# Gate and up projections of a routed feed-forward block: twelve plain products against one step of Strassen's scheme

## What is computed

```python
x = x + tanh(g_xattn) * attention(layernorm(x), ctx, ctx)     # 32 query heads, 8 key heads of 16
x = x + tanh(g_ffn) * ffn(layernorm(x))

# ffn, t = 8192 tokens, h = 512, FS = 1408, 32 experts of F = 352, 4 per token, 64 tokens per expert at most
shared = (silu(x @ Wsg) * (x @ Wsu)) @ Wsd * sigmoid(x @ Wse)
probs = softmax(x @ Wr); topw, topi = top_k(probs, 4), normalised
expert e, on its first 64 tokens: (silu(xe @ Wg[e]) * (xe @ Wu[e])) @ Wd[e], weighted, added to the token's row
```

## Time and profile before

| | |
|---|---|
| runs of the kernel | 2306.56 us median of 3 (2306.51 to 2308.84) |
| the profiled execution, its own time | 2309.02 us |
| its span in the profile | 2307.2 us |
| instructions in the profile | 43358 |

### The profile page before, as it was taken

One profiled execution on the slowest core, in us unless ns is written; L12 is line 12 of the kernel. 1 busy time (PEld: TensorE's weight loads), 2 busy tenths in 40 slices (PEclk: granted clock), 3 DMA queues, 4 the chain that ended last, 5 costly groups with the idle time before them and its releaser, 6 DMA issues.

```text
span 2307.2 us, 43358 instructions
## 1 busy us (share of the span) xinstructions
PE 2250.8 (98%) x13953; PEld 1735.8 (75%) x13953; DVE 1150.2 (50%) x2218; ACT 763.7 (33%) x1312; POOL 593.1 (26%) x1395
## 2 busy tenths in 40 slices
PE   6999999999997999999999999999999999999999
PEld 5777777777776877777777777778777777777777
DVE  6999999999997723222232222223222232223232
ACT  5888888888883101010110101101010110101010
POOL 5677777777763100000000000000000000000100
PEclk9999999999998999999999999999999999999999
DMA  3555555555553133222223221222222223222321
GB/s 83 147 146 144 146 146 150 144 144 146 143 159 127 10 120 118 85 84 80 65 94 107 84 80 64 80 81 101 84 84 80 68 93 105 84 80 92 121 67 43
DMA packets 269455, 235.14 MB, mean 102 GB/s; under 512 B 120545, under 2 KB 196321, under 8 KB 269410
## 3 DMA queue, kind: packets, MB, share of 16 engines
q1 hardware_dynamic: 265058, 221.89, 32.0%
q0 software_dynamic: 4352, 12.65, 1.9%
HBM read 161.88 MB, written 71.57 MB: 101 GB/s over the span
## 4 chain that ended last, share of the span: by engine, by line
PE 68%; DVE 1%; DMA 0%; issue 0%; DVEq 0%; POOLq 0%
PE acc L1128 7%; PE p_u L1144 7%; PE p_u L1145 7%; PE p_u L1146 7%; PE acc L1130 7%; PE acc L1129 7%; PE p_g L1144 7%; PE p_g L1146 7%; PE p_g L1145 7%; PE p_x L1176 2%; PE p_y L1163 2%; PE p_x L1163 2%; PE p_x L1154 0%; DMA rows<-out_dram 0%; PE p_y L1169 0%; DVE rows L1108 0%
## 5 line engine op out<-in xcount | busy, mean ns | idle before, releaser
L1062 DVE TENSOR_TENSOR act_f<-p_u,act_f 128x512 f32<-128x512 f32 x176 | 121.7, 692 | 984.9 <-PE p_u L1146 984.8
L967 ACT ACTIVATE act_f<-p_g 128x512 f32<-128x512 f32 x176 | 105.3, 598 | 1215.8 <-PE p_g L1146 1194.8
L561 DVE TENSOR_REDUCE negmax<-p_max 128x8 f32<-128x1024 f32 x256 | 312.6, 1221 | 43.6 <-PE p_max L713 43.6
L1128 PE MATMUL acc<-wd_h,hh 128*128 128x512 f32 x704 | 279.5, 397 | 0.0
L1144 PE MATMUL p_u<-xh,wgu_h 128*128 128x512 f32 x704 | 274.8, 390 | 3.6 <-DVE act_f L1062 3.6
L1144 PE MATMUL p_g<-xh,wgu_h 128*128 128x512 f32 x704 | 275.7, 392 | 0.0
L1145 PE MATMUL p_u<-xl,wgu_h 128*128 128x512 f32 x704 | 274.6, 390 | 0.0
L1146 PE MATMUL p_u<-xh,wgu_l 128*128 128x512 f32 x704 | 274.4, 390 | 0.0
L1129 PE MATMUL acc<-wd_l,hh 128*128 128x512 f32 x704 | 274.3, 390 | 0.0
L1130 PE MATMUL acc<-wd_h,hl 128*128 128x512 f32 x704 | 274.2, 390 | 0.0
L1146 PE MATMUL p_g<-xh,wgu_l 128*128 128x512 f32 x704 | 274.2, 390 | 0.0
(11 more groups left out here) (142 smaller groups left out, 3465.5 us busy)
## 6 DMA issues: line engine op xcount, KB each, us to landing
ew<-in_L_ffn_Wg_dram SPq DMA_DIRECT2D x32, 704.0 KB
ew<-in_L_ffn_Wu_dram SPq DMA_DIRECT2D x32, 704.0 KB
xs<-in_x_dram SPq DMA_DIRECT2D x64, 256.0 KB, 2.7
xres<-in_x_dram SPq DMA_DIRECT2D x64, 256.0 KB, 2.8
out_dram<-x SPq DMA_DIRECT2D x64, 256.0 KB, 2.7
xn_rows<-xn SPq DMA_DIRECT2D x64, 256.0 KB, 3.0
xn_cols<-xnT SPq DMA_DIRECT2D x64, 256.0 KB, 3.3
rows<-out_dram SPq DMA_DIRECT2D x16, 1024.0 KB, 5.2
```

The costliest lines, as they stand in the source:

```text
L561: nc.vector.tensor_reduce(negmax[c // 2][:, :].rearrange("p (g c i) -> p c i g", g=2, c=2)[:, c % 2, :, :], p_max[:, :, :].rearrange("p a ...
L1062: nc.vector.tensor_tensor(act_f[:, :], p_u[:, :], act_f[:, :], ALU.mult).then_inc(h_done, 1)
L1128: mm(acc[:, j, :], a[:, t], wd_h[:, f, :], start=(f == 0), stop=False)
```

## The change

Gate and up are taken together as one product of 2x2 blocks: the weights are four blocks (rows: first and second half of the 512 inputs; columns: gate and up), and so are the tokens (features in halves, tokens in halves of 256). Instead of the eight block products (12 + 12 matmuls of 512 columns per chunk) seven are made, with sums of blocks (the Winograd form of Strassen's step):

- weights: A11, A12, A21, A22 and S3 = A11-A21, S1 = A21+A22, S2 = S1-A11, S4 = A12-S2; seven blocks are kept (S1 takes A21's place), each split in high and low;
- tokens: B11, B21, B22 and T1 = B12-B11, T3 = B22-B12, T2 = B22-T1, T4 = B21-T2, each split in high and low.

Each product has 2 contraction blocks x 3 terms = 6 matmuls of 256 columns. The outputs are completed partly by accumulation in PSUM and partly by copies on ScalarE (`term`, `sum16`) and additions on VectorE. The seven split weight blocks need more SBUF, so only 5 chunks of them are made in the first stage; the second stage becomes two passes over the 16 tiles (32 tile bodies), 5 chunks in the first pass and 6 in the second, whose weights are loaded and split between and beside the passes. Rows and tokens are loaded twice, rows stored twice. The down product of all chunks of a tile now comes at the tile's end, bank by bank, with two banks. Experts start in tile 4; a pair is multiplied in one tile and its rows are added in the next, one pair per two tiles until the last six tiles.

```diff
--- before.py
+++ after.py
+NF = (5, 6)
-WCH = FS // (NB // 2)
+WA = 128 * NF[0]
+WCH = WA // (NB // 2)
+ORDER = (B11, B21, T2, T1, T3, B22, T4)
...
+                def weight_sums(pair):
+                    def w(c):
+                        return wst[:, c, :, :]
+                    pool.wait_ge(wst_in, 32 * (pair + 1))
+                    alone(pool, spare_p)
+                    chain.inc(nc.gpsimd.tensor_tensor(w(S3), w(A11), w(A21), ALU.subtract))
+                    chain.wait(pool)
...
+                    nc.gpsimd.tensor_tensor(w(S4), w(A12), w(S2), ALU.subtract).then_inc(wsum_done, 1)
...
                     if (B - 5).ok:
                         take_top(B - 5)
+                    if weights_split(B):
+                        weight_sums(B.pair)
                     if (B + 2).ok:
                         inverse_root(B + 2, stat1, mv1, ve1, rs1, qraw_done, rs1_done)
...
                     if weights_split(B):
-                        act.wait_ge(wst_in, 32 * (B.pair + 1))
-                        nc.scalar.activation(w_cols(wgu_h, B.pair), wst_cols, ACT.Copy).then_inc(whi_done, 1)
+                        act.wait_ge(wsum_done, B.pair + 1)
+                        nc.scalar.activation(w_cols(ws_h, B.pair), wst_cols, ACT.Copy).then_inc(whi_done, 1)
```

TensorE in the second stage (the old chunk loop and `down` fall away):

```diff
+                def product(T, f, bank, a, b, start):
+                    w_h, w_l = w_slot(T.part, f)
+                    if f == 0:
+                        pe.wait_ge(xlo_done, NX * T.n + ORDER.index(b) + 1)
+                    for k in range(2):
+                        mm(bank, w_h[:, a, k, :], x_h[:, b, k, :], start=start and k == 0, stop=False, skip_group_check=not start)
+                        mm(bank, w_h[:, a, k, :], x_l[:, b, k, :], start=False, stop=False, skip_group_check=not start)
+                        last = mm(bank, w_l[:, a, k, :], x_h[:, b, k, :], start=False, stop=(k == 1), skip_group_check=not start)
+                    return last
+                def last_two(T, f):
+                    s = T.step + f
+                    pe.wait_ge(p5_done, s + 1)
+                    product(T, f, p_c[:, 0:HT], S4, B22, False).then_inc(c12_mm, 1)
+                    pe.wait_ge(c22_done, s + 1)
+                    product(T, f, p_a[:, (T.flip + f) % 2, 0:HT], A22, T4, False).then_inc(c21_mm, 1)
...
+                    for f in range(T.nf):
+                        wait(pe, h1_done, s - 1)
+                        product(T, f, bank, A11, B11, True).then_inc(p1_mm, 1)
+                        wait(pe, c11_done, s)
+                        product(T, f, p_b[:, 0:HT], A12, B21, True).then_inc(c11_mm, 1)
+                        if f > 0:
+                            last_two(T, f - 1)
+                        pe.wait_ge(p1_done, s + 1)
+                        product(T, f, bank, S2, T2, False).then_inc(x16_mm, 1)
+                        wait(pe, c12_done, s)
+                        product(T, f, p_c[:, 0:HT], S1, T1, True).then_inc(p5_mm, 1)
+                        pe.wait_ge(x16_done, s + 1)
+                        product(T, f, bank, S3, T3, False).then_inc(c22_mm, 1)
...
+                    wait(pe, add_done, TB * T.n - 1)
+                    down(T, 0, range(0, 2))
+                    last_two(T, end)
+                    down(T, 0, range(2, end))
+                    wait(pe, add_done, TB * T.n)
+                    down(T, 1, range(0, 2))
+                    down(T, 0, range(end, T.nf))
+                    down(T, 1, range(2, T.nf))
+                    for j in range(2, TB):
+                        pe.wait_ge(add_done, TB * T.n + j - 1)
+                        down(T, j, range(T.nf))
```

ScalarE and VectorE in a chunk, and VectorE at a tile's end:

```diff
+                        nc.scalar.activation(term[:, :], p_a[:, (T.flip + f) % 2, 0:HT], ACT.Copy).then_inc(p1_done, 1)
+                        if f > 0:
+                            silu(T, f - 1, 1)
+                        act.wait_ge(x16_mm, s + 1)
+                        wait(act, c12_done, s)
+                        nc.scalar.activation(sum16, p_a[:, (T.flip + f) % 2, 0:HT], ACT.Copy).then_inc(x16_done, 1)
...
+                        nc.scalar.activation(term[:, :], p_c[:, 0:HT], ACT.Copy).then_inc(p5_done, 1)
+                        if f > 0:
+                            high(T, f - 1)
+                        silu(T, f, 0)
...
+                        nc.vector.tensor_tensor(gate[:, 0:HT], p_b[:, 0:HT], term[:, :], ALU.add).then_inc(c11_done, 1)
+                        if f > 0:
+                            products(T, f - 1)
+                        work(T, f, e, adds)
+                        nc.vector.tensor_tensor(up2, bank, term[:, :], ALU.add).then_inc(c22_done, 1)
+                        if f > 0:
+                            low(T, f - 1)
...
+                    add_acc(T, 0)
+                    if not T.last:
+                        dve.wait_ge(xb_in, 32 * (T.n + 1))
+                        two_sums(n, low_block, low_block(T1))
+                        x_low(n, 0, low_block)
+                        four_sums(n, low_block)
+                    add_acc(T, 1)
+                        for j in range(1, NX):
+                            x_low(n, j, low_block)
+                    if T.at(0, NT - 1):
+                        wide_low(1)
+                    add_acc(T, 2)
+                    if T.at(0, NT - 1):
+                        wide_low(2)
+                    add_acc(T, 3)
```

More of the change, by code:

```diff
@@ L756, in part @@
                 return ew[:, at[0] - n:at[0]]
-            wraw = [part(2 * E) for i in range(2)]
             first = part(CAP)
@@ L818, in is_first, with two @@
-            def is_first(i):
-                return isinstance(i, int) and i == 0
+                def two(part, m, p):
+                    for j in range(2):
+                        t = Tile(part, 2 * m + j)
+                        t.flip = j * t.nf % 2
+                        pair = Pair(p, 0, 1, 2, 4) if j == 0 and p is not None else None
+                        body(t, pair, p if j == 1 else None)
+                two(0, 0, None)
+                two(0, 1, None)
+                two(0, 2, 0)
@@ new lines, in tiles @@
+                with eng.Fori(3, NT // 2 - 1) as m:
+                    two(0, m, m - 2)
+                two(0, NT // 2 - 1, 5)
+                two(1, 0, 6)
+                with eng.Fori(1, 5) as m:
+                    two(1, m, m + 6)
+                two_last = [(10, Pair(11, 0, 1, 2, 4), None), (11, Pair(12, 2, 3, 4, 5), 11), (12, Pair(13, 2, 3, 4, 5), 12),
+                            (13, Pair(14, 2, 3, 4, 5), 13), (14, Pair(15, 2, 3, 4, 5), 14), (15, None, 15)]
+                for i, pair, adds in two_last:
+                    body(Tile(1, i), pair, adds)
@@ L845, in body @@
+                def body(T, pair, adds):
+                    end = T.step + T.nf
+                    if T.at(0, 0):
+                        for s in range(NF[0]):
+                            load_down(s, s)
                         sp.wait_ge(zeros_set, 1)
                         sp.dma_start(xn_dram[TOK:TOK + 1, :], zeros).then_inc(route_out, 16)
-                        sp.wait_ge(key_mm, 1)
-                        load_x(1)
-                        sp.wait_ge(xlo_done, KC)
-                        load_rows(0)
@@ L915, in expert @@
                 def expert(p, rows_before, more):
+                    if more:
+                        gather_x(p + 1)
                     for h in range(2):
@@ L957, in body, with high @@
+                def high(T, f):
+                    s = T.step + f
+                    act.wait_ge(h2_done, s + 1)
+                    if f == 0:
+                        wait(act, acc_mm, TB * T.n)
+                    nc.scalar.activation(hh[:, f, :], act_g, ACT.Copy).then_inc(hh_done, 1)
+                def body(T, pair, adds):
+                    if T.at(0, 0):
+                        split_x(0, first_block)
                         act.wait_ge(key_mm, 1)
-                        for q in range(4):
-                            nc.scalar.activation(keys[:, 512 * q:512 * q + 512], acc[:, q, :], ACT.Copy).then_inc(key_done, 1)
+                        for q, bank in enumerate((acc[:, 0, :], acc[:, 1, :], p_x[:, :], p_y[:, :])):
+                            nc.scalar.activation(keys[:, 512 * q:512 * q + 512], bank, ACT.Copy).then_inc(key_done, 1)
@@ L986, in _ @@
+                    silu(T, T.nf - 1, 1)
+                    high(T, T.nf - 1)
+                    if not T.last:
+                        split_x(T.n + 1, low_block)
+                    if T.at(0, NT - 1):
+                        wide_high(1)
+                        wide_high(2)
                 tiles(act, body)
```

670 lines of the change are left out of this document (406 added, 264 removed).

## The result

The changed kernel takes **2324.01 us** (median; 2320.94 to 2325.56), the kernel before beside it on the same chip 2307.7: a ratio of 1.0069 with the interval 1.0051 to 1.0086. It is slower by 16 us, less than one per cent, but the interval lies wholly above 1. The forecast was 2289, faster by 18, with a range of 2275 to 2302 and a wider one that ended at 2322; the result lies above both. The profiled execution took 2320.9 us, its span 2319.1, which is 11.9 more than the span before.

What follows compares the result with a forecast made beforehand. It took TensorE as the bound, by pure matmul issue in the second stage, with VectorE nearly as busy in the first. Terms -82+38+9+2+3+8+5 = -17 us took 2309.0 to 2292, as a median 2289 us, range 2275 to 2302.

Steps and rivals of the forecast that it cites:

- Once only: Switch between passes: low parts delay VectorE's additions, ScalarE awaits down weights, +8 us; opening: operations ahead of VectorE's chunk work, +5.
- The step: Gate and up products, second stage: 42 matmuls of 256 columns per chunk at 0.1185 us each, a gain of 82 us.
- The first stage: Four dependent GpSimd weight sums ahead of the inverse roots delay VectorE's xn in each second batch, +38 us.
- Inside a chunk: Gate and up chunks: ScalarE's copy of X16 reaches TensorE slightly late for C22, 0.05 us in 176 chunks, +9 us.
- tiles' ends: End of tiles with five chunks: the next tile's token split just fits beside the down matmuls, +2 us over 16 tiles.
- gathers: Expert rows added one tile later: their gather lands late for VectorE in chunk 1, 0.2 us in 16 tiles, +3 us.
- rival 3: Inside chunks, the X16 copy comes behind another ScalarE instruction and TensorE waits; 2333 us at 0.3 per chunk, chance 0.24.
- Rival 4: Over the whole kernel, the forecast's small terms reach their upper ends; 2302 to 2311 us, chance 0.13.
- Rivals 1 and 2: First-stage VectorE stand is absorbed, 2261 us, chance 0.15; matmul step scales with columns in a long stream, 2251, chance 0.04.

Runs made afterwards that it cites:

- run 8: The kernel of run 7 with the switch's two wide low parts back on VectorE, behind its last addition of the first pass; 2273.72 us, ratio 0.9852.
- run 9: The kernel of run 8 with GpSimd also holding back the sums of the third and later weights until that addition; 2277.17 us, ratio 0.9862.
- Run 5: The changed kernel with ScalarE's early work reordered in the opening, separate waits per down weight, and wide-weight work moved to tile 5; 2318.41 us.
- run 6: The changed kernel with ScalarE's roundings reordered at the switch, wide low parts given to GpSimd, and separate waits per down weight; 2320.25 us.
- run 7: The changed kernel with weight sums behind the inverse roots and the new orders of the opening and the switch together; 2281.73 us, ratio 0.9893.
- Run 4: The changed kernel with two of three terms of every gate and up product cut from 256 to 192 columns; 2298.97 us in a single run.
- runs 1 to 3: The kernel before with four unused GpSimd sums, ahead of the inverse roots 2345.53 us, behind them 2312.06; the changed kernel with its sums behind them 2288.91.

## Why the prediction was wrong

By its own terms, in the profiled executions: -17 was summed, +12 came. The step that failed is **"Once only"**, the opening and the switch. Beside it the matmul step was mis-sized.

- **Once only** (+5 and +8, upper ends 10 and 14). Measured about 28 - 3 = 25 and 17: 42 us instead of 13, 29 more, as much as the whole distance between sum and result (the other misses cancel). I counted operations that VectorE has ahead of its chunk work, and left three things out. ScalarE's program order puts key copies, exponentials and weight roundings ahead of the copy that TensorE needs next. One wait was put ahead of all down products instead of one for each weight. And I priced VectorE's work without GpSimd's beside it: in the changed kernel a sum of 0.42 us takes 4.07 in the opening, and the six low parts at the switch take 5.36 us as in run 8, 3.69 in run 9. Run 5 took 5.6 us back at the opening. At the switch run 6 has no gain that is shown (three waits went and one of the same size came), and run 8, which took that one out, lies 8.0 us under run 7. From the changed kernel to run 8 the second stage fell by 12.5 us, from 1563.8 to 1551.3. So where the 42 us lie is measured, and the cause is shown by experiment for a part of them; for the rest it is read from the timelines. Some waits that each run removed came back at another place, so a sum over waits overstates what mending one gives.
- **The step**, 0.1185 taken, 0.120 measured, the upper of the two readings of the earlier trace rows: 11.4 us less gain. The average of two readings with so few intervals was no better than either, and 7392 matmuls multiply it. Run 4 and the transposes show why half of the long step (0.1133) was out of reach: there is a floor of about 0.11 per matmul, just under the 0.120 of 256 columns.
- **The first stage**, +38: 33.6 measured, and shown by runs 1 to 3 to be the sums' place ahead of the roots. The mechanism was right; that the number came so near is partly luck. The stand was 1.2 and not 1.55 us, in part because a dependent sum takes 0.45 and not 0.52; not 0.8 but all of it reached the period (22.43 instead of 21.23); and it came in 28 pairs, not 32.
- **Inside a chunk, tiles' ends, gathers** (+9, +2, +3): about 7 us of excess in all instead of 14. TensorE's waits on copies between 1080 and 1440 us are 0.4 us in all, so rival 3, to which 0.24 was given for "slower", is false: it ended slower by another road, that no rival had. Rival 4 comes nearest, since it lets the small terms reach their upper ends, but the once-only term went far past its own (25 and 17 us against 10 and 14).
- Rivals 1 and 2 are out: the stand was not absorbed, and the step does not scale with the columns. By the gap formula of the Trainium skill ("TensorE: Matmul & The Clock Gate", section "Back-to-back issue gap"), which it gives for a single matmul by itself, the step would be an estimated 109 ns; 120 were measured in the stream.

The sum of the misses: 11.4 on the step, 29 once only, -7 on the small terms, -4 on the first stage, is 29, from -17 to +12.

**Still open.** Of the 42 us some 26 remain in run 8 by the same count: 17 in the first four tiles, 9 at the switch. I did not try to take the routing rounds (2.29 us each) out of the first chunks, nor the copies between TensorE's products. That the floor of about 0.11 does not come from the columns is shown by the transposes; that it is the weight load was not measured by itself and is argued. That GpSimd and VectorE exclude each other is shown by durations that match: the two of 4.4 us go when GpSimd's part moves (run 8), and the one of 4.07 goes along when GpSimd's subtraction moves from tile 1 to tile 5 (run 5). Which resource they share, no run shows; only the section of the Trainium skill named at run 7 says it.

## What to carry to other kernels

A change that wins in a steady loop is decided at its edges: walk each engine's program order through the first and last turn and ask what stands ahead of the one instruction the bounding engine waits for. Small dependent operations belong behind whatever another engine waits for, even if they are nearly free by themselves: here the place of four of them was worth 35 us. Before work is given to GpSimd, look what VectorE does at that time: here a two-input operation there cost the sum of both, not the longer.

## What the runs showed of the hardware

- A VectorE operation with two SBUF inputs can last as long as the GpSimd operation that it meets (0.69 us became 4.39 and 4.44 beside 4.40, 0.42 became 4.07 beside 4.06), and the other way round (GpSimd's sum 0.74 became 2.45 beside a VectorE low part of 2.02).
- Matmuls with new 128x128 weights each step by 0.109 us at 128 columns (transposes), 0.120 at 256, 0.2267 at 512, and by 0.1145 in the mean at 256, 192, 192. So two matmuls of 256 columns cost 0.240 where one of 512 costs 0.227.
- In TensorE's waits of 2.3 to 5.0 us, or just behind them, the granted clock fell to the 1.2 GHz level for 3.4 to 10.2 us at a time, which adds 0.095 us to the step of a 256-column matmul in it. Of the 10.2 us at the switch TensorE waited 3.8; the other 6.4 are some 30 matmuls, near 3 us on top of what the view of waits shows.
